# A graph layer and a 64-expert layer on one core: three gather buffers instead of four, part of one turn's down-projection kept on chip, and the up-projections of turns 0 and 1 one matrix at a time

## What is computed

```python
x = x + relu(segment_sum(edge_weight * (layernorm(x) @ W)[src], dst) + bias)
xt = layernorm(x)
w, idx = top_k(sigmoid(xt @ Wg.T + bg), 2); w = w / w.sum(-1)
nx = layernorm(xt)
h1 = (gamma[e] * nx + beta[e]) @ W1[e] + b1[e]      # 512 -> 256, for each expert e
h3 = (gamma[e] * nx + beta[e]) @ W3[e] + b3[e]
y = sum over the token's two experts: w[e] * ((silu(h1) * h3) @ W2[e] + b2[e])   # 256 -> 512
z = (silu(nxs @ Ws1 + bs1) * (nxs @ Ws3 + bs3)) @ Ws2 + bs2, nxs = nx * gs + bs
x = x + y + z
```

## Time and profile before

| | us |
|---|---|
| time, median of 3 runs (lowest, highest) | 422.3 (422.23, 423.02) |
| time of the profiled execution | 422.33 |
| its span, from the first instruction to the last | 420.6 |
| PE busy in the span | 394.2 (94%) |
| DVE, ACT, POOL busy | 212.9, 156.4, 174.7 |

### The profile page before, as it was taken

How to read it: one execution, slowest core, us unless ns; L and a number is a source line. 1 busy time by engine, 2 the same in 40 slices (tenths; PEclk the granted TensorE clock), 3 DMA queues, 4 the chain that set the end, 5 groups by cost and what they waited for, 6 DMA issues and landing times.

```text
span 420.6 us, 6394 instructions
## 1 busy us (share of the span) xinstructions
PE 394.2 (94%) x1892; PEld 205.2 (49%) x1893; DVE 212.9 (51%) x698; ACT 156.4 (37%) x388; POOL 174.7 (42%) x276
## 2 busy tenths in 40 slices
PE   6898999999999998999999999999997999878985
PEld 5556777755565556634344344344442434333332
DVE  8899999325566677552342332432423234223346
ACT  8677788313223121133233233232332123231231
POOL 2679998313655575712332332322313223121100
PEclk9999999999999998999999999999999899999998
DMA  7999977230000936299999999999999999999888
GB/s 259 213 341 407 406 270 287 57 124 25 27 25 27 325 126 229 57 401 412 405 401 407 408 407 406 407 406 405 406 407 408 407 408 406 404 407 409 337 291 321
DMA packets 44023, 129.15 MB, mean 307 GB/s; under 512 B 7747, under 2 KB 8963, under 8 KB 43859
## 3 DMA queue, kind: packets, MB, share of 16 engines
q1 hardware_dynamic: 38242, 120.45, 75.4%
q0 software_dynamic: 5744, 8.28, 5.5%
HBM read 119.64 MB, written 17.85 MB: 327 GB/s over the span
## 4 chain that ended last, share of the span: by engine, by line
PE 78%; DVE 6%; DMA 5%; issue 4%; POOL 4%; SPq 1%; ACT 1%; DVEq 0%; POOLq 0%; ACTq 0%
PE bank L1521 26%; PE bank L1384 13%; PE bank L1553 12%; PE bank L1543 5%; DMA w<-in_L_ffn_W_dram 5%; PE bank L1333 4%; PE bank L1509 4%; PE bank L1306 3%; PE bank L1372 2%; PE bank L1405 2%; POOL M L515 1%; POOL AT L515 1%; PE bank L1653 1%; PE bank L1278 1%; PE bank L1393 1%
## 5 line engine op out<-in xcount | busy, mean ns | idle before, releaser
L1165 DVE SCALAR_TENSOR_TENSOR osl<-bank,b13T,osl 128x64 f32<-128x64 f32 x128 | 27.6, 277 | 145.5 <-ACT osl L760 140.5
L1521 PE MATMUL bank<-w,xhT 128*64 128x512 f32 x352 | 80.6, 599 | 4.2 <-issue 3.1
L753 ACT COPY xh<-bank 128x512 f32<-128x512 f32 x33 | 19.3, 585 | 128.9 <-PE bank L1521 125.9
L1384 PE MATMUL bank<-HW,AT 128*128 128x512 f32 x128 | 58.3, 593 | 0.0
L611 POOL DMA_INDIRECT totals<-GW,A x16 | 16.4, 1025 | 79.3 <-PE bank L1509 64.3
L1521 PEld LDWEIGHTS bank<-w,xhT 128*64 128x64 f32 x352 | 23.7, 137 | 45.1 <-issue 40.9
L611 POOL DMA_INDIRECT totals<-osl,A x16 | 16.4, 1026 | 70.5 <-PE bank L1509 61.7
L1553 PE MATMUL bank<-w,osl 128*64 128x512 f32 x184 | 43.8, 594 | 0.5 <-DVE osl L1165 0.5
L607 POOL DMA_INDIRECT A<-nx_rows,A x33 | 34.0, 1031 | 12.5 <-issue 12.5
L1384 PEld LDWEIGHTS bank<-HW,AT 128*128 128x128 f32 x128 | 22.9, 192 | 21.0 <-issue 21.0
L660 ACT ACTIVATE osl<-iota,eT 128x128 f32<-128x128 f32 x90 | 27.8, 388 | 10.2 <-PE bank L1333 10.2
(11 more groups left out here) (246 smaller groups left out, 595.8 us busy)
## 6 DMA issues: line engine op xcount, KB each, us to landing
w<-in_L_ffn_W_dram SPq DMA_DIRECT2D x67, 1024.0 KB, 19.3
A<-in_L_ffn_W_dram SPq DMA_DIRECT2D x15, 1024.0 KB, 19.8
HW<-in_L_ffn_W_dram SPq DMA_DIRECT2D x8, 1024.0 KB, 18.5
totals<-w SPq DMA_DIRECT2D x1, 4096.0 KB, 27.1
AT<-in_L_ffn_W_dram SPq DMA_DIRECT2D x4, 1024.0 KB, 20.0
w<-totals SPq DMA_DIRECT2D x8, 512.0 KB, 7.0
kept_up<-in_L_ffn_W_dram SPq DMA_DIRECT2D x2, 1024.0 KB, 10.1
out_dram<-X SPq DMA_DIRECT2D x8, 256.0 KB, 4.2
```

Source lines behind the costliest of these rows:

```text
L1165: ins = v.scalar_tensor_tensor(hT[b][:, m, CAP * h:CAP * h + CAP], bank[4][:, (HC + m) * P + CAP * h:(HC + m) * P + CAP * h + CAP], b13T[: ...
L1384: ins = t.matmul(bank[4 + s % 2][:, :], AT[:, s % 2, k, :], HW[:, k, :], start=(k == 0), stop=(k == NB - 1))
L1521: ins = t.matmul(bank[2 + b][CAP * h:CAP * h + CAP, :], xe[b][:, c, CAP * h:CAP * h + CAP], weights[:, h, :, c, :], start=(c == 0), stop=( ...
```

## The change

There are three edits.

1. `XG` and `AHEAD` go from 4 to 3. The three gather buffers lie in `R`, in `M` and in `A`; two of those are free by then. Some small tables move from `M` to `eT`.
2. The space in `A` that this frees (6 KiB per partition) takes `kept_down`: three quarters of turn 24's down-projection. Two transfers, of 4 KiB and 2 KiB per partition (512 and 256 KiB), are issued right after slot 4 is filled in the first part. In the loop, turn 24's down load shrinks from 1 MiB to 256 KiB (`load_second_down`), and `down` of turn 24 reads three of its four blocks from `kept_down`.
3. Turns 0 and 1 do all of `up` with W1 first, then all with W3 (`up_by_kind`): 16 matmuls of 256 columns in place of 8 of 512. A new semaphore `h1_ps` tells SP when the W1 half is done, and SP then issues the W1 load of turn 6 (7), and the W3 load after the second half.

```diff
-XG, AHEAD = 4, 4
+XG, AHEAD = 3, 3
+BY_KIND = 2
...
+        kept_down = A[:, SLOT:SLOT + (HC + 1) * D]
+        xg = [R[:, :, :].rearrange("p c n -> p (c n)"), M[:, 0, :, :].rearrange("p a b -> p (a b)"), A[:, o:o + 512]]
...
+            def load_kind(j, v, k):
+                sp.dma_start(of_kind(up_flat[v], k), (W1v, W3v)[k][:, 2 * j:2 * j + 2, :]).then_inc(w13_in[v], 16)
...
+            def load_second_down(j, v):
+                sp.dma_start(down_flat[v].rearrange("p (e n) -> p e n", e=2)[:, 1, D:], W2v[:, 2 * j + 1, D:]).then_inc(w2_in[v], 16)
...
                     load_down(RING // 2, RING // 2)
+                    sp.dma_start(kept_down[:, 0:HC * D], W2v[:, 2 * pair_of(KEPT), :]).then_inc(kept_down_in, 16)
+                    sp.dma_start(kept_down[:, HC * D:], W2v[:, 2 * pair_of(KEPT) + 1, 0:D]).then_inc(kept_down_in, 16)
...
+                if j < BY_KIND:
+                    sp.wait_ge(h1_ps, j + 1)
+                    load_kind(pair_of(j + SLOTS), j, 0)
                 sp.wait_ge(h_ps, j + 1)
-                if j + SLOTS == EX:
+                if j < BY_KIND:
+                    load_kind(pair_of(j + SLOTS), j, 1)
+                elif j + SLOTS == EX:
...
+                    elif j + SLOTS - 1 == KEPT:
+                        load_second_down(pair_of(KEPT), KEPT % SLOTS)
...
+            def up_by_kind(j, weights):
+
+                for k in range(2):
+                    if k and j == 0:
+                        pe.wait_ge(xg_in[1], 16)
+                        pe.wait_ge(z_added, 2)
+                        turn_rows(1, 1)
+                    for c in range(DC):
+                        if not k and j == 0 and c == DC // 2:
+                            pe.wait_ge(xe_ready, 1)
+                        for h in range(2):
+                            ins = t.matmul(bank[2 + j][CAP * h:CAP * h + CAP, HID * k:HID * k + HID], xe[j][:, c, CAP * h:CAP * h + CAP],
+                                           weights[:, h, k, c, :], start=(c == 0), stop=(c == DC - 1), skip_group_check=True)
+                    ins.then_inc(h_ps if k else h1_ps, 1)
...
-                                       down_w[v][:, h, m, :], start=(m == 0), stop=(m == HC - 1))
+                                       down_w[v][:, h, m, :] if kept is None or h * m else kept[:, HC * h + m, :], start=(m == 0), stop=(m == HC - 1))
```

More of the change, by code:

```diff
@@ L180, in moe_gnn @@
         OS = EX % SLOTS
-        xg = [A[:, SLOT + 512 * i:SLOT + 512 * i + 512] for i in range(XG)]
-        o = SLOT + 512 * XG
+        kept_down = A[:, SLOT:SLOT + (HC + 1) * D]
+        kept_down_w = kept_down.rearrange("p (m d) -> p m d", d=D)
+        o = SLOT + (HC + 1) * D
+        xg = [R[:, :, :].rearrange("p c n -> p (c n)"), M[:, 0, :, :].rearrange("p a b -> p (a b)"), A[:, o:o + 512]]
+        o += 512
         TOK = A[:, o:o + PAIRS].bitcast(i32)
@@ L196, in moe_gnn @@
         Lspread = xg[XG - 1][0:PAIRS, 2 * CAP * REC:4 * CAP * REC].rearrange("j (a p) -> j a p", a=REC)
-        tables = M[:, 0, 2:4, :].rearrange("p a n -> p (a n)")
+        tables = eT[:, 0:2, :].rearrange("p a n -> p (a n)")
         count = tables[0:64, 0:1]
@@ L247, in moe_gnn @@
         x_in = [sem(f"x_in{i}") for i in range(5)]
-        late_in, kept_in = sem("late_in"), sem("kept_in")
+        late_in, kept_in, kept_down_in = sem("late_in"), sem("kept_in"), sem("kept_down_in")
         consts = sem("consts")
@@ L301, in moe_gnn @@
             "xe_ps", "xe_ready", "h_ps", "h_copied", "hT_ps", "sl_ready", "hT_ready", "y_ps", "y_ready"))
-        xe_first = sem("xe_first")
+        xe_first, h1_ps = sem("xe_first"), sem("h1_ps")
         list_spread = sem("list_spread")
@@ L350, in of_kind @@
                 return a.rearrange("p (e k n) -> p e k n", e=2, k=2)[:, :, k, :]
+            def load_kind(j, v, k):
+                sp.dma_start(of_kind(up_flat[v], k), (W1v, W3v)[k][:, 2 * j:2 * j + 2, :]).then_inc(w13_in[v], 16)
             def load_up(j, v):
-                for k, W13v in enumerate((W1v, W3v)):
-                    sp.dma_start(of_kind(up_flat[v], k), W13v[:, 2 * j:2 * j + 2, :]).then_inc(w13_in[v], 16)
+                for k in range(2):
+                    load_kind(j, v, k)
+            def load_second_down(j, v):
+                sp.dma_start(down_flat[v].rearrange("p (e n) -> p e n", e=2)[:, 1, D:], W2v[:, 2 * j + 1, D:]).then_inc(w2_in[v], 16)
             def load_down(j, v):
@@ L1510, in turn_rows, with up @@
                 ins.then_inc(xe_ps, 1)
-            def up(b, weights, first=False):
+            def up(b, weights):
                 for c in range(DC):
[L1515 to L1519, removed]
                     for h in range(2):
@@ L1544, in turn_hidden, with down @@
                 ins.then_inc(hT_ps, 1)
-            def down(j, b, v, between=None):
+            def down(j, b, v, between=None, kept=None):
                 pe.wait_ge(hT_ready, j + 1)
@@ L1561, in down_of @@
                 pe.wait_ge(w2_in[j % SLOTS], 16 * (j // SLOTS + 1))
-                if j != EX:
+                if j == KEPT:
+                    pe.wait_ge(kept_down_in, 32)
+                    down(j, j % 2, j % SLOTS, between, kept_down_w)
+                elif j != EX:
                     down(j, j % 2, j % SLOTS, between)
@@ L1603, in _ @@
                     pe.wait_ge(h_copied, j - 1)
-                if j != EX:
-                    up(j % 2, up_w[j % SLOTS] if j != KEPT else kept_w, j == 0)
+                if j < BY_KIND:
+                    up_by_kind(j, up_w[j])
+                elif j != EX:
+                    up(j % 2, up_w[j % SLOTS] if j != KEPT else kept_w)
                 else:
```

## The result

The changed kernel takes 451.97 us (median of 4 runs, 450.11 to 456.9) against 422.66 for the kernel before beside it: a ratio of 1.0682, 95% interval 1.0654 to 1.0711. The forecast was 440.0, between 433 and 455. The time lies in the range and on the side forecast, 12 us above the value. (Ratios here leave out runs that lie more than 1.5% above the fastest of the same kernel; of these four that is the one of 456.9.)

What follows compares the result with a forecast made beforehand. The weight stream bounds the kernel before, PE close behind; the change makes late gathers the bound. Turn 31's `up` 16.2 us later on 422.33 gives 438.5; one clock fall, 1.7, gives 440.2, forecast 440, range 433 to 455.

Steps and rivals of the forecast that it cites:

- The link: Turns: gather issued 8.67 us into a pass lands 6.3 later, needed after 12.92; two passes take 15.0, 13 times, 195.0 us.
- The clock: PE in the turns: one new wait passes 2 us and the clock falls once, 1.7 us; bounds 0 and 14 falls.
- rival C: PE in the turns: clock falls after most of the 14 longer waits, 24 us on top, 462 us; chance 0.07.
- the range's upper bound: Whole kernel, 455 us: landings at 6.9 add 7.8, first part at its bound 0.8, four more clock falls 6.8.
- the 0.9 us that I added for the extra matmuls of turns 20, 22 and 24: PE in those turns' passes: one more pair of matmuls each, 0.86 us, adding 0.9 to the slower interleaved chain.
- The list heads: First part: two new transfers delay SP's load of the list heads, so turn 0 comes 1.1 us later; bounds 0 and 1.9.
- The kept down-projection and the halves: Weight stream in the turns: 1.9 us less DMA time and a start up to 2.5 us sooner, both buying nothing.
- rival A: Turns: gathers land in 2.7 to 3.2 us, PE never waits, stream stays the bound; 3.3 us faster, 419.0; chance 0.10.
- far bound of 4.4 us: PE in turns 0 and 1: 32 extra weight loads of 0.137 us if nothing hid them; the forecast took nothing.
- The stream's end: DMA engines at the end of the turns: done near 394 us, long before PE's last `up`.
- B: Turns: gathers land about 5.0 us after issue, new waits just eat PE's 9.7 us of room; chance 0.09.

Runs made afterwards that it cites:

- square of buffers and turns ahead: XG and AHEAD varied: kernel before (4, 4); from it 3, 3: 450.74 us and 4, 3: 454.03; changed kernel with 3, 4: 419.53, without halves 421.15.
- four transposes: Changed kernel with four extra identity transposes (about 0.6 us) on PE ahead of the wait for the gather, passes 4 to 29: 447.2 us, median of four.
- an eighth: Changed kernel with the loop's weight loads fetching only an eighth of each matrix's columns: 411.73 us, one execution.
- half: Changed kernel with the loop's weight loads fetching half of each matrix's columns: 419.21 us, one execution.

## Why the prediction was right, and what was off

**The link (right).** Every step from the pass's start to the next gather is in the timeline as foretold: 8.84 us to the issue (8.67 forecast), and in the 13 gathers of the chain 5.9 to 7.6 us from issue to PE, by the mean 6.5 (6.3 forecast). PE waits at `turn_rows` and no more at `up`. The square of buffers and turns ahead shows that the place in POOL's program is the cause; the first edit alone gave a ratio of 1.0647, the whole change 1.0682.

**The clock (mis-sized).** This is the step that failed in size: "I count one such fall, 1.7 us". There were five in the profiled execution, 8.5 us. The price of one was right; the point from which it comes was not. I took it to be about 2 us, since waits of 1.45 to 1.8 us had left the clock alone. Two of the five waits, 2.14 and 2.54 us, lie above that, so the spread brought two where I counted one; the other three falls came behind 1.52, 1.75 and 1.81 us, and with four transposes behind 1.45 and 1.70, while waits of 1.47, 1.55 and 1.58 had none. So there is no sharp length between 1.45 and 1.8, and rows without a fall didn't exclude one. Five of the eight waits over 1.4 us had a fall: that is rival C's "most of the longer waits", but of eight where C had 14. That the time still lies in the range is owed to the range's upper bound, which had room for four more falls.

**The rest of the miss is the link's length, about 3 us, and the other runs' clock.** The profiled execution, 450.11 us, is the fastest of the four; the others had a lower mean clock (0.970, 0.968 and 0.965 against 0.975), which goes with the 1.9 us from there to the median. In the profiled one, pass 3 started at 193.45 (193.9 forecast), pass 29 at 400.99 (389.8). Of the 11.6 us by which these 26 passes took longer, 8.5 are the falls; 3.1 over 13 links are 0.24 us each, which the two terms above (0.17 and 0.2) more than cover; the 0.9 us that I added for the extra matmuls of turns 20, 22 and 24 falls out, since from pass 15 on the chain's links start in odd passes. The run with four transposes and a clock of 1.000 is in line with this: 442.03, against 438.5 forecast without a fall.

**The list heads (no effect; the number was near by luck).** I counted 1.1 us. SP's load of the list heads starts at 151.83, POOL's scatter then waits 1.11 us for it, and the first gather follows at 168.18:

```profile
136.70 0.90 SPq L357 DMA_DIRECT2D A<-in_L_ffn_W_dram  x2
...
151.83 0.69 SPq L405 DMA_DIRECT2D A<-slots  x1
...
154.25 1.11 POOL L567 DMA_INDIRECT slots<-small,GW  x1 [1.11 <-DMA A<-slots]
...
168.18 1.09 POOL L626 DMA_INDIRECT R<-nx_rows,A  x1 [3.02 <-issue]
```

The first gather was at 167.3 before, 0.9 us sooner, but here slot 4's fill, which stands ahead of the new transfers in SP's program, is later too: 136.70 against 135.94. From that fill to the first gather it is 31.5 us against 31.4. The load of the lists stands 0.9 us further behind the fill (15.13 us against 14.22), and that was absorbed before POOL's work for block 7: from the load's start to POOL's scatter it took 2.42 us instead of 2.87, POOL's second record scatter was 0.34 us shorter, and the 0.21 us of waiting went. In six other traces of kernels with both new transfers and three gathers ahead of the loop, the first gather stands at 167.15 to 167.98, so executions of the same first part differ by as much as the 1.1 us in question.

**The kept down-projection and the halves (right that they buy nothing here).** Without them the time was 450.74, with them 451.97. They couldn't show while the gather was the bound. With the gather in time they give 3.0 us together, as against 3.3 in rival A's sum. The halves cost PE nothing, which excludes the far bound of 4.4 us.

**The stream's end (off).** I had it near 394; it is between 400 and 401. SP refills a slot only when PE has used it, so passes of 7.9 us (220.6 us from pass 3 to pass 31, 28 passes) feed the stream late as well: 390 GB/s from 185 to 345 us. It changes no sum, since nothing waits for weights.

**Rivals A and B.** Their condition is gathers that land sooner, and the lighter loads met it: under about 4.1 us with an eighth, where PE did not wait, and about 5 us in the chain with half, where its waits were short. Under the full stream the condition wasn't met. The times, 411.73 and 419.21, are no test of A's 419.0, since these runs load fewer weights.

## What to carry to other kernels

- Count the turns ahead of a prefetch by where its issue stands in the issuing engine's program: "three ahead" behind a scatter that itself waits a pass for its data was only two passes. The order of issue can be kept when a buffer is taken away; three buffers with four ahead, with both other edits, took 0.9929 of the time before.
- When a wait is forecast that returns in every pass, price the clock with every one of them and not with the longest: here waits from 1.5 us on cost a further 1.7 us each time the clock fell behind one, five times in eight over 1.4 us.
- A shared stream has two sides: it makes the landing of a small transfer long (6.3 us instead of 2.9), and a late small transfer slows the stream in return (390 GB/s instead of 406 from 185 to 345 us), because slots come free later.

## What the hardware showed that was not expected

- The same program, run four times on one chip, took 442.03 to 450.81 us, in step with its mean granted clock (1.000 to 0.979). Three buffers and three ahead alone does the same: 447.77 and 448.30 us at 0.991 and 0.984, 453.19 and 453.77 at 0.972. The kernel before goes less plainly with its clock: 421.99 us at 0.985 and 422.93 at 0.999, among 17 runs of one round from 421.29 to 425.73.
- In the 12 us in which turns 0 and 1, taken by halves, release four loads of 1 MiB one by one, the DMA engines count as 97% busy and move 354 GB/s, where the loaded turns show 405 at 1.03. Why a share that is 6% lower moves 13% less isn't shown.
